# Placement of the TensorE transposes in the self-attention stage of a decoder kernel

## The reference

```
x = x + self_attn(layernorm(x))          # the part that the change touches
x = x + cross_attn(layernorm(x), ctx)    # 16 heads, 128 context rows
x = x + ffn(layernorm(x))                # 512 -> 64, hinges, 64 -> 512
```

## Time and profile before

| | |
|---|---|
| Three timed runs | 1964.53, 1967.95, 1969.17 us |
| The profiled execution: its own time, its span | 1966.47 us, 1964.7 us |
| Mean granted TensorE clock over the span | 0.945 |
| Busy share of the span: PE, PEld, DVE, ACT, POOL | 87%, 72%, 80%, 51%, 52% |
| From 240 to 670 us (nine of the loop's steps): PE busy | 430.0 of 430 us |
| One step of the loop | 47.3 us |
| Products of Q, K and V (line 557): 2304 matmuls | 550.4 us busy |
| Output projections of the self stage (line 630): 768 matmuls | 191.4 us busy |

### The profile page before, as it was taken

One profiled execution on the slowest core, in us unless ns is written; L12 is line 12 of the kernel. 1 busy time (PEld: TensorE's weight loads), 2 busy tenths in 40 slices (PEclk: granted clock), 3 DMA queues, 4 the chain that ended last, 5 costly groups with the idle time before them and its releaser, 6 DMA issues.

```text
span 1964.7 us, 39568 instructions
## 1 busy us (share of the span) xinstructions
PE 1717.4 (87%) x14022; PEld 1421.1 (72%) x14022; DVE 1563.5 (80%) x2292; ACT 999.5 (51%) x3134; POOL 1018.0 (52%) x739
## 2 busy tenths in 40 slices
PE   3399999999999999945899998988997989889975
PEld 2387888888888888834777777777776777767764
DVE  3568888888888888773689887887887878878874
ACT  2232223323232322211687776776776767767771
POOL 4126676666666676653365443653455435644422
PEclk8699999999999999977899999998998989989997
DMA  5201111111111111032110111101110111101101
GB/s 194 91 22 44 43 44 43 43 43 43 43 43 43 43 43 44 22 96 72 40 41 24 51 57 58 62 19 58 57 56 20 56 58 57 62 14 57 40 18 43
DMA packets 55172, 98.30 MB, mean 50 GB/s; under 512 B 5184, under 2 KB 12480, under 8 KB 54976
## 3 DMA queue, kind: packets, MB, share of 16 engines
q1 hardware_dynamic: 53104, 94.12, 14.1%
q10 hardware_dynamic: 1872, 1.66, 0.3%
HBM read 58.80 MB, written 36.96 MB: 49 GB/s over the span
## 4 chain that ended last, share of the span: by engine, by line
PE 30%; DVE 14%; issue 6%; ACT 3%; POOL 1%; DVEq 1%; POOLq 0%; ACTq 0%
PE ring L1177 18%; PE sc L1205 4%; PE ring L1272 3%; DVE ntop L1382 3%; DVE stats_c L1420 2%; DVE x2T L1349 2%; ACT prob_c L1309 2%; PE ring L1230 1%; DVE stats L1389 1%; PE sc L1197 1%; PE ring L1182 1%; DVE x L1403 1%; DVE pT L1349 1%; DVE x L1439 1%; DVE xT_c L1349 1%
## 5 line engine op out<-in xcount | busy, mean ns | idle before, releaser
L557 PE MATMUL qb<-wqkv,xT 128*128 128x512 f32 x2304 | 550.4, 393 | 0.0
L557 PEld LDWEIGHTS qb<-wqkv,xT 128*128 128x128 f32 x2304 | 428.8, 188 | 87.0
L1309 ACT ACTIVATE prob_c<-sc,ntop 128x128 f32<-128x128 f32 x1024 | 361.6, 390 | 155.5 <-DVE ntop L1382 155.5
L1132 POOL TENSOR_TENSOR rstd<-vare,half_c 128x1 f32<-128x1 f32 x64 | 35.0, 547 | 467.1 <-DVE vare L1396 467.1
L1177 PE MATMUL ring<-wqkv,aT_c 128*128 128x512 f32 x768 | 202.1, 414 | 39.7 <-DVE x L1403 39.7
L1309 ACT ACTIVATION_READ_ACCUMULATOR prob_c<-sc,ntop 128x1 f32 x1024 | 235.7, 230 | 0.0
L505 POOL TENSOR_TENSOR prod_pool<-v,prob 128x1024 f32<-128x1024 f32 x64 | 174.8, 2732 | 85.6 <-DVE prob L796 80.4
L1382 DVE TENSOR_REDUCE ntop<-sc 128x4 f32<-128x512 f32 x256 | 170.3, 688 | 51.6 <-PE sc L1205 38.1
L672 ACT ACTIVATE qk<-qb 128x512 f32<-128x512 f32 x128 | 76.4, 597 | 263.1 <-PE qb L557 263.1
L630 PE MATMUL ob<-wout,aT 128*128 128x512 f32 x768 | 191.4, 399 | 10.7 <-DVE aT L826 10.7
L1177 PEld LDWEIGHTS ring<-wqkv,aT_c 128*128 128x128 f32 x768 | 145.8, 197 | 75.6 <-DVE x L1403 36.0
(11 more groups left out here) (133 smaller groups left out, 3226.2 us busy)
## 6 DMA issues: line engine op xcount, KB each, us to landing
x_tile<-in_x SPq DMA_DIRECT2D x16, 1024.0 KB, 5.3
x_scratch<-xres SPq DMA_DIRECT2D x16, 1024.0 KB, 4.3
x_tile<-x_scratch SPq DMA_DIRECT2D x16, 1024.0 KB, 7.8
out<-x SPq DMA_DIRECT2D x64, 256.0 KB, 2.0
kt<-k_scratch SPq DMA_DIRECT2D x16, 512.0 KB, 3.3
v_c<-v_scratch SPq DMA_DIRECT2D x16, 256.0 KB, 3.8
raw<-in_wqkv SPq DMA_DIRECT2D x3, 1024.0 KB, 14.9
ctx<-in_ctx SPq DMA_DIRECT2D x1, 1024.0 KB, 7.8
```

Source lines behind the costliest of these rows:

```text
L557: last = nc.tensor.matmul(qb[g % 4][:, :], xT[p][a][:, k, t * P:(t + 1) * P], wqkv[b][:, k, c * D:(c + 1) * D], start=(n == 0), stop=(n == ...
L1309: last = nc.scalar.activation(prob[:, h, :], sc[g][:, (h % 4) * C:(h % 4 + 1) * C], ACT.Exp, bias=ntop[:, h:h + 1], accum_out=total[:, t % ...
```

## The change

`products` gets an argument `beside`, a function that is called behind each block k of three products. `transpose_row`, which issued four transposes in a row, becomes `transpose_block`, which issues one. So the four transposes of X0 to X3 now stand inside G4 to G7, one behind each three products, and A0 to A3 stand in the same way inside G8 to G11. The waits of a row stay with its first transpose (k = 0) and its semaphore with its last (k = 3). The order of the groups changes with it: O0 comes behind G9, O1 behind G10, and O2 and O3 both behind G11. No instruction is added or taken away, and the lists of the other engines are the same.

```diff
-                for k in range(DK):
-                    for a, b in PASSES:
-                        last = nc.tensor.matmul(...)
-                        n += 1
-                last.then_inc(qkv_psum, 1)
+                for k in range(DK):
+                    if has(j):
+                        for n, (a, b) in enumerate(PASSES):
+                            last = nc.tensor.matmul(...)
+                        if k == DK - 1:
+                            last.then_inc(qkv_psum, 1)
+                    if beside:
+                        beside(t, k)
...
-                def xn_T(t):
+                def xn_T(t, k):
...
-                    wait(pe, xn_done, R * (j + 1) + t + 1)
                     n = TB_TURNS.index(("x", t))
-                    turn_free(n)
-                    transpose_row(n % 2, xn, t).then_inc(xt_psum, 1)
+                    if k == 0:
+                        wait(pe, xn_done, R * (j + 1) + t + 1)
+                        turn_free(n)
+                    last = transpose_block(n % 2, xn, t, k)
+                    if k == DK - 1:
+                        last.then_inc(xt_psum, 1)
...
                 for t in range(R):
-                    products(j, p, R + t)
-                    xn_T(t)
-                attn_T(0)
-                products(j, p, 8)
-                attn_T(1)
+                    products(j, p, R + t, xn_T)
+                products(j, p, 8, attn_T)
+                products(j, p, 9, attn_T)
                 output_projection(j, 0)
-                products(j, p, 9)
-                attn_T(2)
+                products(j, p, 10, attn_T)
                 output_projection(j, 1)
-                products(j, p, 10)
-                attn_T(3)
+                products(j, p, 11, attn_T)
                 output_projection(j, 2)
-                products(j, p, 11)
                 output_projection(j, 3)
```

More of the change, by code:

```diff
@@ L545, in _, with products, transpose_block @@
         def _(pe):
-            def products(j, p, g):
-                if not has(j):
-                    return
+            def products(j, p, g, beside=None):
                 c, t = g // R, g % R
[L551 to L554, removed]
+                if has(j):
+                    if c == 0:
+                        wait(pe, xt_lo, R * j + t + 1)
+                    wait(pe, qkv_sb, N_QKV * j + g - 3)
                 for k in range(DK):
-                    for a, b in PASSES:
-                        last = nc.tensor.matmul(qb[g % 4][:, :], xT[p][a][:, k, t * P:(t + 1) * P],
-                                                wqkv[b][:, k, c * D:(c + 1) * D],
-                                                start=(n == 0), stop=(n == 11))
-                        n += 1
-                last.then_inc(qkv_psum, 1)
-            def transpose_row(bank, src, t):
-                for k in range(DK):
-                    last = nc.tensor.transpose(tb[bank][:, k * P:(k + 1) * P], src[:, t, k * P:(k + 1) * P],
-                                               ident[:, :])
-                return last
+                    if has(j):
+                        for n, (a, b) in enumerate(PASSES):
+                            last = nc.tensor.matmul(qb[g % 4][:, :], xT[p][a][:, k, t * P:(t + 1) * P],
+                                                    wqkv[b][:, k, c * D:(c + 1) * D],
+                                                    start=(k == 0 and n == 0), stop=(k == DK - 1 and n == 2))
+                        if k == DK - 1:
+                            last.then_inc(qkv_psum, 1)
+                    if beside:
+                        beside(t, k)
+            def transpose_block(bank, src, t, k):
+                return nc.tensor.transpose(tb[bank][:, k * P:(k + 1) * P], src[:, t, k * P:(k + 1) * P], ident[:, :])
             def step(j, p):
@@ L578, in turn_free, with attn_T @@
                         wait(pe, xt_lo, R * (at + 1) + t + 1) if has(at, 1) and not is_step(at, -2) else None
-                def attn_T(t):
+                def attn_T(t, k):
                     if not has(j, -1):
@@ L584, in attn_T @@
                     a = j - 1
[L585 to L588, removed]
                     n = TB_TURNS.index(("a", t))
-                    turn_free(n)
-                    transpose_row(n % 2, attn, t).then_inc(at_psum, 1)
-                def xn_T(t):
+                    if k == 0:
+                        if t < 2:
+                            wait(pe, attn_dve, 2 * a + t + 1)
+                        else:
+                            wait(pe, attn_pool, 2 * a + t - 1)
+                        turn_free(n)
+                    last = transpose_block(n % 2, attn, t, k)
+                    if k == DK - 1:
+                        last.then_inc(at_psum, 1)
+                def xn_T(t, k):
                     if not has(j, 1):
                         return
-                    wait(pe, xn_done, R * (j + 1) + t + 1)
                     n = TB_TURNS.index(("x", t))
-                    turn_free(n)
-                    transpose_row(n % 2, xn, t).then_inc(xt_psum, 1)
+                    if k == 0:
+                        wait(pe, xn_done, R * (j + 1) + t + 1)
+                        turn_free(n)
+                    last = transpose_block(n % 2, xn, t, k)
+                    if k == DK - 1:
+                        last.then_inc(xt_psum, 1)
                 for g in range(4):
```

## The result

The changed kernel took 1986.87 us, the median of six runs (1982.13 to 1987.58), beside 1966.30 us for the kernel before (six runs, 1963.91 to 1969.43). The ratio is 1.0096, with a 95% interval of 1.008 to 1.0113: slower by 19 us (the medians lie 20.6 apart). Forecast were 1984 us and slower. The six runs fall into two groups by their mean granted clock: two took 1982.13 and 1982.46 us at 0.947, and four took 1986.69 to 1987.58 us at 0.941 or 0.942.

The account below looks back on a forecast made before the run. PE bounds the loop now, PE and DVE together after the change. Terms 7.3 + 4.8 + 1.1 + 2.9 = +16.1 us on 1966.47 give 1982.6, predicted as a median of 1984; own range 1976 to 1992, over all 1971 to 2000.

Parts of the forecast that it names:

- The price of a lone transpose: Transposes alone between products: 0.125 us against 0.117 in a row, 0.008 more for each of 368, +2.9 us.
- The rival price of 0.067: Rival: the product's load is hidden too, so a lone transpose costs 0.067 us and the kernel takes 1963; chance 0.09.
- The wait in the loop: PE waits 0.73 us at X2 for x_lo(0) in each of ten loop steps (3 to 12), +7.3 us.
- The later entry of DVE: With O3 directly behind O2, DVE enters each next step 0.50 us later, so x_lo(0) ends 18.54 after G0.
- DVE does not come later: Rival: DVE's end of the step is 0.50 shorter, the loop's wait 0.23 us, the time 1977.5; chance 0.13.
- Steps 2, 13 and 14: Written-out steps: X2 waits 2.38 us and A0's wait of 0.78 goes, 3 x (2.38 - 0.78) = +4.8 us.
- Step 1: X2 already waits 1.71 us; the full 2.04 is added and A0's wait goes, +1.1 us.
- Step 0: First step: there is slack, so no wait was added; only 16 transposes at the lone price.
- POOL did not get in first in the loop: Rival: POOL starts before DVE's small instruction in ten more steps, 1.65 us each, 2000.5 in all; chance 0.07.
- the weight loads were not hidden further ahead: Rival: a product's weight load hides behind the product ahead of the lone transpose, making that transpose cheap; chance 0.09.
- The sum: Whole kernel: 7.3 + 4.8 + 1.1 + 2.9 = +16.1 us on the profiled execution's 1966.47 us.
- The range: The forecast's own range: 1976 (transpose price 0.108) to 1992 (price 0.145); over all, 1971 to 2000.

Follow-up runs that it names:

- e4_lo_early: Changed kernel with DVE's x_lo(0) put ahead of the last addition of the weighting for t = 1, x_lo(1) directly behind it; ratio to before 1.0008.
- e2_a_alone: Kernel before with only A0 to A3 alone inside G8 to G11 and the change's order of O; X rows of four as before; ratio 0.9997.
- e1: Kernel before with only X0 to X3 standing alone inside G4 to G7; A rows of four and O groups in their old places; ratio 1.0056.
- e5: Kernel before with the change's order of groups alone: rows of four, A0 to A3 behind G8 to G11, O2 and O3 at the end; ratio 0.9986.
- e7: Kernel before with the change's order of groups and DVE's x_lo(0) and x_lo(1) moved forward, transposes in rows of four; ratio 0.9972, 1961.54 us.
- e6: Kernel before with only DVE's x_lo(0) and x_lo(1) moved forward; ratio 1.0.
- e3: Changed kernel with transposes in pairs behind the sixth and twelfth product of a group instead of one behind each third; ratio to before 1.0028.

## Why the prediction was right, step by step

- **The price of a lone transpose.** Taken at 0.125 against 0.117 in a row, 0.008 more; measured 0.009 in e4_lo_early and 0.012 in e2_a_alone. The distance that the forecast named as its sign, from the product ahead of a lone transpose to the second product behind it, is 299.88 - 299.30 = 0.58 us: two products (0.454) and 0.12. The rival price of 0.067 is excluded. The reading of the earlier trace rows, one weight load under way ahead, holds for a transpose alone, by the loads at 299.54 and 299.65.
- **The wait in the loop.** Forecast was a step of 48.2; measured 48.10. The wait was forecast too long. The later entry of DVE was put at 0.50 and is 0.34, because `take_x1(3)` starts 0.08 after `vare` does (287.62, 287.70) and not behind its end, and `a_lo(3)` starts 0.93 after A3's last transpose, not 0.99. The wait at X2 is then 0.51 to 0.57 us in the ten steps, where the forecast had 0.73, less the 0.06 that the slower X0 and X1 take up.
- **Both moves count.** Without the order of O (e1) the loop waits 0.17 and without the earlier X2 (e2, e5) not at all. The forecast's 0.23 for "DVE does not come later" is e1's case.
- **Steps 2, 13 and 14.** Forecast +1.8 each, measured 1.59, 1.62 and 1.65: again the entry of DVE. A0's wait went, as said.
- **Step 1, the term that was mis-sized.** It was put at +1.1 and the transposes' price, 1.3; it is +3.2. The wait grew by 2.3, as forecast in kind (2.04), and 0.3 more because `x_lo(0)` ended 22.0 after G0 and not 21.7. Left out was the fall of the clock behind a wait of 4.0 us: X2 to X3 took 1.5 us more at the lower level.
- **Step 0** is 1.0 longer and was forecast as 0.1. In it the lower clock of the start lasts longer (from 101.3 to 103.4 us the granted clock is 0.50, before 0.99). Since e5 and e7, whose X rows are as before, have it too (36.64, 36.76) and e2 and e6 have not (35.59, 35.20), lone transposes are not needed for it; what decides it stays open.
- **The rivals.** POOL did not get in first in the loop (line 770 takes 0.17 there as before), and the weight loads were not hidden further ahead.
- **The sum.** Forecast were +16.1; measured are 15.7 in the profiled execution, 19 by the ratio and 20.6 between the medians. That the sum came so near is in part luck. By place, the waits with the price of the transposes, forecast and measured are: the loop 9.2 and 8.0; steps 2, 13 and 14 together 5.4 and 4.9; step 1 1.3 and 3.2; step 0 0.1 and 1.0; steps 15 and 16 0.1 and 1.0; the cross stage 0 and -2.5. So the terms that were too large and the shorter cross stage cover for the left-out clock and the starting step. The self stage alone lost 18.2 us. The medians lie further apart than the profiled executions because four of the six launches took some 5 us longer than the profiled one, at the lower mean clock; none of the four was profiled, so where in the launch they lose it stays open, and no launch took the 1984 that was forecast.
- **The range.** Its lower end of 1976 does not follow from the price of 0.108: 368 x (0.125 - 0.108) = 6.3 us below 1984 is 1978.

## What to carry to other kernels

A move of work on the busiest engine must be priced at the waits that stand with it: the first instruction of a row carries the wait for its buffer, and spreading the row forward brings that wait forward by as much as it spreads, here 2.04 us against a slack of 1.95. Before spreading, list for each such wait how long before its use the releaser ends, and follow the releaser's engine once around the step, since two moves can add up on one slack: the new order of O, harmless by itself, made the loop's wait three times as long (0.17 us in e1, 0.51 in the changed kernel). Where the wait cannot be avoided, try moving the small releasing instruction ahead in its own engine's list. That gave back 17 of 19 us here and cost nothing in the loop (e6: 47.29 as before); with rows of four and the new order of O it beat the kernel before. It pays only where the wait stands, and the next wait behind must be looked at too: in step 1 of e6, A0 took over the whole wait of X2.

## What the runs showed of the hardware that was not expected

After PE had stood still for 4.0 us (changed kernel, step 1), for 3.3 us (e3, step 1) and for 2.64 us by the bracket, 2.8 in starts (e6, step 1), the granted clock fell to the lower level for a while: it was 0.57 from 158 to 162 us in the changed kernel and in e3, and 0.51 from 161.9 to 165.3 us in e6. After 1.71 us at the same place in the kernel before it was 1.00 (157 to 161 us), and after 2.00 us in step 13 of the changed kernel too (740 to 744 us). Taking away one of the longer waits can thus give back more than the wait: here 1.5 us, what X2 to X3 took more at the lower level.

One more transpose in a row costs 0.108 us; a transpose costs 0.117 in rows of four, 0.126 to 0.129 alone. Pairs did not halve what is paid over rows of four: a step costs 0.21 us more for 9 more places where transposes stand between products, and 0.28 for 25 more. The price of such a place is therefore not one fixed number, and what else is in it these runs do not tell.
